# Level 0's odd map with rows of 33 elements in place of 36, in a small U-Net on one Trainium2 core

## The reference

```
def basic_block(x, w1, w2, stride=1, ds=None):
    out = relu(conv3(x, w1, stride) * BN_S)
    out = conv3(out, w2, 1) * BN_S
    identity = conv1x1(x, ds, stride) * BN_S if ds is not None else x
    return relu(out + identity)
x = basic_block(x, e0b0c1, e0b0c2)      # level 0
x = basic_block(x, e0b1c1, e0b1c2)      # level 0
f0 = x
x = basic_block(x, e1b0c1, e1b0c2, stride=2, ds=e1b0ds)   # level 1, then the rest
```

## Time and profile before

| | |
|---|---|
| median of 3 runs | 91.72 us |
| the profiled execution | 91.77 us |
| its span, first to last instruction | 89.9 us |
| TensorE, busy | 83.3 us (93%) |
| VectorE, busy | 64.0 us (71%) |
| ScalarE, busy | 44.8 us (50%) |
| GpSimd, busy | 27.5 us (31%) |
| mean granted TensorE clock | 0.983 |

### The profile page before, as it was taken

How to read it: one execution, slowest core, us unless ns; L and a number is a source line. 1 busy time by engine, 2 the same in 40 slices (tenths; PEclk the granted TensorE clock), 3 DMA queues, 4 the chain that set the end, 5 groups by cost and what they waited for, 6 DMA issues and landing times.

```text
span 89.9 us, 1557 instructions
## 1 busy us (share of the span) xinstructions
PE 83.3 (93%) x541; PEld 74.4 (83%) x541; DVE 64.0 (71%) x189; ACT 44.8 (50%) x94; POOL 27.5 (31%) x43
## 2 busy tenths in 40 slices
PE   5988999999999999999999999999999999999900
PEld 3666999998777789999977777999999999887600
DVE  5569999799968799755644559999637798543650
ACT  6006114778445065754423159999920079990410
POOL 7300060999920000555440000300694001500140
PEclk9999999999999999999999999999999999999985
DMA  1879920054674003560000000000000000000075
GB/s 26 245 239 299 293 94 0 0 116 105 178 208 114 19 7 112 161 188 5 0 0 0 0 0 4 0 0 0 0 7 0 4 0 0 7 0 0 0 257 210
DMA packets 4183, 6.51 MB, mean 72 GB/s; under 512 B 464, under 2 KB 2128, under 8 KB 4176
## 3 DMA queue, kind: packets, MB, share of 16 engines
q1 hardware_dynamic: 4032, 6.29, 23.5%
q10 hardware_dynamic: 144, 0.13, 0.4%
HBM read 5.37 MB, written 1.05 MB: 71 GB/s over the span
## 4 chain that ended last, share of the span: by engine, by line
PE 85%; DMA 4%; DVE 3%; SPq 1%; ACT 1%; POOLq 1%; issue 1%
PE psum L838 79%; DMA x_sb<-x_in 4%; PE psum L877 2%; PE psum L975 2%; SPq L418 1%; POOLq L167 1%; PE psum L1030 1%; PE psum L863 1%; DVE stats L612 1%; DVE moments L627 1%; DVE shared L641 1%; ACT result L587 0%; ACT shared L584 0%; PE psum L870 0%; DVE flat L749 0%
## 5 line engine op out<-in xcount | busy, mean ns | idle before, releaser
L470 POOL TENSOR_TENSOR odd<-relu,odd 128x363 fp32r<-128x363 f32 x12 | 13.4, 1131 | 16.0 <-ACT odd L545 16.0
L838 PE MATMUL psum<-shared,w_e0b0c 128*128 128x364 f32 x72 | 12.5, 332 | 0.4 <-DVE shared L641 0.4
L838 PEld LDWEIGHTS psum<-shared,w_e0b0c 128*128 128x128 f32 x72 | 12.0, 188 | 0.7 <-issue 0.7
L838 PE MATMUL psum<-shared,w_e0b1c 128*128 128x364 f32 x72 | 12.2, 329 | 0.0
L838 PEld LDWEIGHTS psum<-shared,w_e0b1c 128*128 128x128 f32 x72 | 12.1, 188 | 0.1
L838 PE MATMUL psum<-odd,w_e0b0c 128*128 128x512 f32 x48 | 12.0, 411 | 0.0
L838 PE MATMUL psum<-odd,w_e0b1c 128*128 128x512 f32 x48 | 12.0, 411 | 0.0
L764 DVE SCALAR_TENSOR_TENSOR relu<-psum,inside 128x363 f32<-128x363 f32 (+2 forms) x18 | 8.7, 488 | 3.8 <-PE psum L838 3.6
L838 PEld LDWEIGHTS psum<-odd,w_e0b1c 128*128 128x128 f32 x48 | 9.1, 190 | 2.6
L838 PEld LDWEIGHTS psum<-odd,w_e0b0c 128*128 128x128 f32 x48 | 9.1, 190 | 2.6
L545 ACT ACTIVATE odd<-relu 128x363 fp32r<-128x363 f32 x12 | 6.2, 519 | 7.0 <-DVE relu L764 7.0
(11 more groups left out here) (126 smaller groups left out, 141.3 us busy)
## 6 DMA issues: line engine op xcount, KB each, us to landing
x_sb<-x_in SPq DMA_DIRECT2D x4, 160.0 KB, 4.0
raw<-e0b0c_in SPq DMA_DIRECT2D x2, 256.0 KB, 4.9
raw<-e0b1c_in SPq DMA_DIRECT2D x2, 256.0 KB, 5.1
raw<-e1b1c_in SPq DMA_DIRECT2D x2, 256.0 KB, 2.7
raw<-e2b1c_in SPq DMA_DIRECT2D x2, 256.0 KB, 2.6
raw<-e1b0c_in SPq DMA_DIRECT2D x1, 448.0 KB, 3.6
raw<-e2b0c_in SPq DMA_DIRECT2D x1, 448.0 KB, 3.8
x_sb<-x_in SPq DMA_DIRECT2D x2, 192.0 KB, 3.9
```

The costliest lines, as they stand in the source:

```text
L470: pool.tensor_tensor(split_of(piece, 1), fp32_of(piece), split_of(piece, 0).bitcast(F32), ALU.subtract).then_inc(lo_ready, 1)
L838: last = pe.matmul(target, w, moving, start=(first and n == 0), stop=(final and n == len(terms) - 1), skip_group_check=skip)
```

## The change

The pitch of a row of `odd0` becomes the 33 elements that are used. A piece of 11 rows is then 363 elements without a gap, for ScalarE's and GpSimd's writes and for GpSimd's read of the high half. TensorE's matmuls still read 16 rows of 32 elements; the distance from one row to the next is 33 elements (132 bytes) where it was 36 (144 bytes). `odd0` takes 17,424 bytes of each partition where it took 19,008, and the tiles behind it move down by 1,568 bytes. No instruction, wait or order is changed.

```
-ODD0_PITCH = 36
+ODD0_PITCH = BLOCKS[0] + 1
```

## The result

| | before | after |
|---|---|---|
| median of 7 runs each | 91.64 us (91.39 to 92.06) | 90.99 us (90.87 to 91.30) |
| ratio, 95% interval | | 0.9929 (0.9904 to 0.9953) |
| profiled execution, span | 91.77, 89.9 us | 90.87, 89.1 us |
| both even stages, start to start | 11.81 + 11.81 us | 11.41 + 11.42 us |

A second measurement of the same kernel (experiment 10) gave 0.9935 (0.9914 to 0.9957).

A forecast was written before the change was run, and what follows sets the result against it. TensorE's matmuls were taken to bound the kernel; writers 0, TensorE's reads +0.26 and tiles behind 0 us gave 91.72 + 0.26 = 92.0 us for the median, range 91.3 to 92.35.

The forecast's parts named there:

- What bounds: From 11.5 to 72.8 us only TensorE's matmuls set the end; other engines' work costs nothing inside its slack.
- The writers: ScalarE's and GpSimd's writes of the odd map, in one run instead of 11 rows: under cover, 0 us.
- TensorE's reads: The 96 even-stage matmuls on the odd map, each row priced by its start modulo 4: +2.7 ns each, +0.26 us.
- a = b = 1: Row starts in classes 2 (a) and 3 (b) modulo 4 cost as much as class 1: 413.9 ns, +0.26 us.
- The unit: In the even stages, a nanosecond on each of the 96 matmuls is 0.1 us of the kernel's time.
- neighbouring rows share a read: Rival at TensorE's read of `odd0`: a row reuses what the last one fetched; -0.34 up to -1.3 us; chance 0.20.
- mild form: Shared reads at `odd0`: rows starting in class 2 or 3 pay nothing; 407.6 ns a matmul, -0.34 us, 91.4.
- a = b = 0: Row starts in classes 2 and 3 modulo 4 cost nothing extra: 407.6 ns a matmul, -3.6 ns, -0.34 us.
- one-run end: Shared reads at `odd0` going through as one run: 397.6 ns a matmul, -13.6 ns, -1.3 us, 90.4.
- The Trainium skill's rule: Memory read in 16-byte lines: a row of 32 covers 8 lines in class 0, 9 otherwise; +0.26 us.
- The tiles behind: `shared`, `relu`, `raw` and the weights moving by 1,568 bytes: 0, with 0.1 us either way.

The follow-up runs named there:

- experiment 10: The changed kernel (pitch 33) as it is, measured again beside a reordered one on the same chip: 0.9935 (0.9914 to 0.9957) of the kernel before.
- experiment 11: Kernel before (pitch 36) with one side copy moved from VectorE to ScalarE, two corner copies and a scaling later: ratio 1.0081 (1.0057 to 1.0105).
- experiment 3: Kernel before, pitch 36 kept, the odd map beginning two elements later: 92.67 us in a single run, matmuls at 421 ns for both shifts.
- experiment 1: Kernel before with pitch 33 and 396 unused elements behind the map, so that no tile behind it moves: 0.9909 (0.9879 to 0.994).
- experiment 9: Changed kernel (pitch 33) with one side copy moved from VectorE to ScalarE, two corner copies and a scaling later: 1.0024 of the kernel before.

## Why the prediction was wrong, step by step

**What bounds.** Right for the stages that the change touches: the 8.2 ns of each of 96 matmuls came off the path. It was not right that the others cost nothing: at 61.2 us the stretch had no slack left against VectorE, and 0.25 us was given back there and behind it.

**The writers.** Right. L545 fell from 520 to 509 ns, as forecast by some 10. L470 went from 915 to 995, inside 850 to 1030, and under its cover; but at pitch 36 it is 983 in experiment 11, so that rise can't be put down to the layout. No gap came at a low half.

**TensorE's reads: the step that failed** is "the mean matmul becomes 404.5 + 12.5 x 4 x (0 + 1 + a + b) / 16". It gives each row a price by its own start, adds the rows to the aligned price of pitch 36, and has no term for the distance between rows. It forecast 413.9 ns for pitch 33, +2.7; measured were 400.3, -10.7 on the 411.0 of the trace before. Pitch 37, with the same starts in the same order and another gap, has a mean of 412.5, and +0.29 us against the forecast's +0.26. So the gap of one element is worth some 12 ns that the formula has nowhere. That a = b = 1 was taken is not what failed: a and b were too small, if anything (1.3, experiment 3), and by the formula that would have made pitch 33 slower by 0.4 us.

**The unit.** The sum multiplies a difference of durations by 96, as if start to start moved alike. It did not: -10.7 ns of duration were -8.2 from start to start, and pitch 37's +1.5 were +3.1. That pitch 37 comes so near to +0.26 us is in part luck.

**The rival** "neighbouring rows share a read" had place and sign, and 0.20. Its mild form was priced too small: it put a = b = 0 on top of pitch 36's aligned price of 404.5 and got 407.6. That base was itself 9 ns above the floor of 395, as the 7 ns to the line of the earlier trace rows had shown. Its one-run end, 397.6 ns, was nearer to the 400.3 than the mild form was. In time the 0.79 us of the stages lie between its -0.34 and its -1.3, and the range went no further than the mild form. Its mechanism is not shown. That sx 0 and sx 1 cost the same at pitch 34, where only with sx 1 rows meet in a group, agrees with a group counted once; a plain price for each idle element says the same.

**The Trainium skill's rule**, "SBUF — State Buffer", Specifications (TRN2), lines of 16 bytes with a price for each crossing, was read as one row at a time. Its width agrees with the runs (starts 2 elements off pay 26 ns at pitch 40, starts 4 off 3 ns). By rows pitch 33 touches 140 lines, and 132 if a line in which two rows meet is counted once; at the fitted 1.2 ns a line that is 10 of the 13.6 ns by which the forecast was off. The rest is the base. Lines alone don't give the price, though: an aligned matmul at pitch 36 touches as many as the one run, 128, and takes 404 ns for 395.

**The tiles behind** were worth nothing (experiment 1), as taken.

**What was not foreseen** is the part given back. VectorE's list at the end of level 0 had no slack in the kernel before: its side copies end at 61.09 us and TensorE's weight load for them starts at 61.21, 0.12 us later, just as with pitch 33, where TensorE plainly waits (60.12 and 60.24). Before, then after; VectorE's low part of the second of the last stage's four pieces, its last side copies, and the weight load:

```profile
52.16 0.90 DVE L794 SCALAR_TENSOR_TENSOR split<-block,split 128x128 fp32r<-128x128 f32 x4 [0.82 <-ACT split L541]
59.80 1.29 DVE L698 CAST shared<-split 32x308 fp32r<-32x308 f32 x4
61.21 0.43 PEld L838 LDWEIGHTS psum<-shared,w_e1b0c 128*128 128x128 f32 x3
```
```profile
51.21 0.90 DVE L794 SCALAR_TENSOR_TENSOR split<-block,split 128x128 fp32r<-128x128 f32 x4 [0.83 <-ACT split L541]
58.83 1.29 DVE L698 CAST shared<-split 32x308 fp32r<-32x308 f32 x4
60.24 0.43 PEld L838 LDWEIGHTS psum<-shared,w_e1b0c 128*128 128x128 f32 x3 [0.24 <-ACT shared L561]
```

From that low part to the end of the side copies it is 61.09 - 52.16 = 8.93 us before and 60.12 - 51.21 = 8.91 after, whatever the matmuls do (8.91 at pitch 34 too). The low part follows the stage's 24th matmul, so it comes sooner by 24 x 8.2 ns = 0.20 us of the stage's 0.39; the other 0.19 is waited for. Pitch 34 bears this out: each stage gains 0.15 us, the half of that is 0.08, and its 15 matmuls take 2.11 us, 0.06 more than before. That VectorE's list makes the gap is shown by experiment 9; this account of its size is read from the traces.

**What stays open.** Why at gaps of four and more the price follows neither the groups nor the gap: pitch 36 aligned 404, 40 aligned 400, 37 and 38 at 412 for either sx, 40 off the boundary 423 to 426. And whether below four it is the group or the idle element that is paid for.

## What to carry to other kernels

When a matmul reads rows with a gap, take the price of one run of the same length as the floor and look at the gap between rows. Here a gap of one float32 cost 5 ns over the floor, one of three as much as the pitch padded to 36, and padding to 36 or 40 made the reads dearer than pitch 33, above all for the half of the shifts that start off a multiple of four elements (417 and 424 ns, where the others take 404 and 400). Price such a layout by the gap as well as by each row's start, and from start to start, not from durations. And where the bound engine gains, look which list of another engine has the least slack at the next place where it is waited for; that sets how much is given back.

## What the runs showed of the hardware

TensorE reading 512 float32r elements as 16 rows of 32: 395 ns in one run, 400, 405 and 411 at gaps of one, two and three elements, 412 at five and six, 400 to 404 at gaps of four or eight if every row starts on a multiple of four elements, and 417 to 426 if every row starts off it.

VectorE's subtraction of two SBUF operands, 128x290, took 0.46 us alone, and 0.63 to 2.55 us when it began under the second of GpSimd's two additions of 2.4 us, ending 0.32 or 0.33 us after it four times out of four. The Trainium skill, "GPSIMD Engine Reference", Key points, names contention with VectorE instructions that have two SBUF inputs. The trace agrees, and shows the form that it takes: the instruction waits. In the changed kernel it begins at 67.62 us, 0.07 after GpSimd's second addition ends at 67.55, so a later scaling or an earlier matmul would walk into it.
